# Moving squares instead of results in a masked depthwise convolution with GDN: denominators in 96x32 column groups

## The reference, cut to what matters

```python
pooled = x.mean(axis=(2, 3))
t = relu(batchnorm(pooled @ w1.T))
wt = (t @ w2.T + b2).reshape(b * 96, 1, 3, 3) * MASK      # rows above, and the pixel to the left
out = depthwise_conv(x, wt, padding=1) + bias             # one 3x3 filter per batch and channel
x2 = out * out
denom_sq = einsum('nchw,ic->nihw', x2, gamma_eff) + beta_eff
result = out * rsqrt(denom_sq)
```

## Time and profile before

| | us |
|---|---|
| median of 3 runs | 260.54 (258.8 to 266.99) |
| the profiled execution's own time | 260.12 |
| its span | 258.2 |
| busy: PE, DVE, ACT, POOL | 199.3, 204.8, 186.3, 169.7 |
| granted TensorE clock, mean | 0.945 |

### The profile page before, as it was taken

One profiled execution on the slowest core, in us unless ns is written; L12 is line 12 of the kernel. 1 busy time (PEld: TensorE's weight loads), 2 busy tenths in 40 slices (PEclk: granted clock), 3 DMA queues, 4 the chain that ended last, 5 costly groups with the idle time before them and its releaser, 6 DMA issues.

```text
span 258.2 us, 2123 instructions
## 1 busy us (share of the span) xinstructions
PE 199.3 (77%) x480; PEld 79.2 (31%) x480; DVE 204.8 (79%) x237; ACT 186.3 (72%) x203; POOL 169.7 (66%) x90
## 2 busy tenths in 40 slices
PE   0024221976999689999969899999698999999973
PEld 0021220322333333434324433333234333433220
DVE  6373239894599985999996699999959999999934
ACT  2220447693799568999974999999689866778472
POOL 2000000039597769899949699999499999999910
PEclk9999999995899959999995999999999999999967
DMA  7999999993429997987999989969835555566584
GB/s 204 243 245 240 243 241 240 244 243 121 143 82 223 309 284 258 300 242 227 262 323 285 274 280 290 271 213 255 307 109 164 176 164 162 150 187 187 148 254 131
DMA packets 13584, 57.63 MB, mean 223 GB/s; under 512 B 2595, under 2 KB 2598, under 8 KB 10886
## 3 DMA queue, kind: packets, MB, share of 16 engines
q1 hardware_dynamic: 13424, 57.22, 78.5%
q10 hardware_dynamic: 150, 0.29, 0.4%
HBM read 26.05 MB, written 25.17 MB: 198 GB/s over the span
## 4 chain that ended last, share of the span: by engine, by line
issue 38%; POOL 32%; DVE 13%; PE 8%; DMA 4%; ACT 2%; POOLq 0%; SPq 0%; ACTq 0%
POOL norm L585 26%; DVE acc L557 8%; POOL sq L574 6%; PE den L519 5%; DVE y L565 4%; DMA out_y<-norm 4%; ACT norm L427 1%; PE den L527 1%; PE acc L500 1%; ACT sq L405 1%; DVE y L567 0%; ACT norm L420 0%; DVE norm L733 0%; PE acc L501 0%; SPq L302 0%
## 5 line engine op out<-in xcount | busy, mean ns | idle before, releaser
L557 DVE SCALAR_TENSOR_TENSOR acc<-ximg,taps,acc 128x1016 f32<-128x1016 f32 x96 | 122.6, 1277 | 26.6 <-ACT acc L398 14.3
L585 POOL TENSOR_TENSOR norm<-y,norm 96x1024 f32<-96x1024 f32 x45 | 105.7, 2361 | 54.3 <-ACT norm L427 54.0
L519 PE MATMUL den<-sq,gam_e 96*96 96x512 f32 x252 | 124.7, 640 | 17.5 <-ACT norm L427 6.7
L427 ACT ACTIVATE norm<-den,beta_e 96x1024 f32<-96x1024 f32 x63 | 69.2, 1102 | 18.4 <-PE den L519 16.6
L519 PEld LDWEIGHTS den<-sq,gam_e 96*96 96x96 f32 x252 | 41.6, 174 | 91.1 <-issue 73.5
L500 PE MATMUL acc<-ximg,diag 128*128 128x512 f32 x108 | 58.3, 622 | 9.6 <-DVE y L567 9.6
L565 DVE SCALAR_TENSOR_TENSOR y<-ximg,taps,acc 128x1016 f32<-128x1016 f32 x48 | 61.1, 1273 | 1.7
L405 ACT ACTIVATE sq<-y 96x1024 f32<-96x1024 f32 x48 | 49.7, 1049 | 10.8 <-DVE y L567 10.7
L585 POOL TENSOR_TENSOR norm<-yd,norm 96x1024 f32<-96x1024 f32 x15 | 35.4, 2359 | 15.7 <-ACT norm L427 15.7
L368 ACT ACTIVATE pool_out<-ximg 128x1920 bf16 (+3 forms) x18 | 34.2, 1902 | 4.0 <-DMA ximg<-in_x 4.0
L574 POOL TENSOR_TENSOR sq<-yd 96x1024 f32<-96x1024 f32 x15 | 28.4, 1892 | 5.8 <-DMA yd<-y 5.8
(11 more groups left out here) (53 smaller groups left out, 46.5 us busy)
## 6 DMA issues: line engine op xcount, KB each, us to landing
out_y<-norm SPq DMA_DIRECT2D x63, 384.0 KB, 3.5
ximg<-in_x SPq DMA_DIRECT2D x12, 816.0 KB, 11.8
ximg<-in_x SPq DMA_DIRECT2D x8, 768.0 KB, 9.7
yd<-y SPq DMA_DIRECT2D x48, 128.0 KB, 3.7
ximg<-in_x SPq DMA_DIRECT2D x12, 272.0 KB, 12.6
ximg<-in_x SPq DMA_DIRECT2D x12, 256.0 KB, 9.7
ximg<-in_x SPq DMA_DIRECT2D x4, 720.0 KB, 6.9
out_y<-norm SPq DMA_DIRECT2D x2, 192.0 KB, 2.4
```

The lines of the kernel that those rows point to most:

```text
L427: nc.scalar.activation(norm[:, g], den[0:C, g % 2], ACT.Abs_reciprocal_sqrt, bias=beta_e[:, 0:1]).then_inc(normed, 1)
L519: ins = nc.tensor.matmul(den[0:C, g % 2, j:j + BANK], gam_e[:, :], sq[:, g, j:j + BANK], start=True, stop=True)
L557: nc.vector.scalar_tensor_tensor(out=tap_to(sums(u, s), tap), in0=tap_in(b, u, s, tap), scalar=tap_w(b, s, tap), in1=tap_to(sums(u, s), ta ...
L585: nc.gpsimd.tensor_tensor(norm[:, g], quarter(u, g), norm[:, g], ALU.mult).then_inc(scaled, 1)
```

## The change: what it does

- ACT squares each result as it stands in its block, on all 128 partitions, into `sq` (now six buffers). `move_d` then moves partitions 96 to 127 of the squares, not of the results, into `sqd`. The results stay where they are.
- The denominators of a block are formed in the block's own layout. For each half of 512 columns there are four matmuls with 32 output channels each: three from `sq` into partitions 0 to 31, 32 to 63 and 64 to 95 of `den`, and one from `sqd` with the 32 channels of this slot into partitions 96 to 127. Each has a weight of 96x32 and reads 512 columns.
- ACT's root (`beta_e` now one column per slot) and POOL's product then work on 128 x 1024 for 48 blocks, instead of 96 x 1024 for 64 quarters. POOL squares nothing. The store of a block is two DMAs, of 384 and of 128 KB.
- The written tables go. Each engine works through the blocks with fixed lags: in step n SP moves block n-1 and stores n-7, ACT squares n-1 and takes the root of n-5, PE forms the denominators of n-4. `norm` has six buffers. The last three products are on DVE. The start, the taps on DVE and the bases are the same work as before.

```diff
+SQUARE_LAG, MOVE_LAG, SUM_LAG, NORM_LAG, STORE_LAG = 1, 1, 4, 5, 7
+POOL_AT = {1: 0, 2: 1, 4: 2, 5: 3, 7: 4, 8: 5}
...
-        yd = sb("yd", [C, 2, N])
-        sq = sb("sq", [C, QUARTERS, N])
-        norm = sb("norm", [C, QUARTERS, N])
-        pool_out = sb("pool_out", [P, 2, (QR - CUT + 1) * W], BF16)
+        sq = sb("sq", [P, 2 * SLOTS, N])
+        sqd = sb("sqd", [C, 2, N])
...
-        beta_e = sb("beta_e", [C, 1])
+        beta_e = sb("beta_e", [P, SLOTS])
...
-        def move_d(sp, b, u, s):
-            sp.wait_ge(convolved, 2 * conv_no(b, u, s) + 2)
-            sp.dma_start(yd[s * CD:(s + 1) * CD, u % 2], y[C:P, u % 2, s]).then_inc(d_moved[u % 2], 16)
-        def store(sp, b, u, g):
-            sp.wait_ge(scaled, norm_no(b, u, g) + 1)
-            sp.dma_start(out_rows(b, u, g), norm[:, g]).then_inc(stored[g], 16)
...
+        def move_d(sp, n):
+            t, s = divmod(n, SLOTS)
+            sp.wait_ge(squared, n + 1)
+            if t >= 2:
+                sp.wait_ge(summed, (t - 2) * SLOTS + SLOTS)
+            sp.dma_start(sqd[s * CD:(s + 1) * CD, t % 2], sq[C:P, pair(n) * SLOTS + s]).then_inc(d_moved[t % 2], 16)
...
+        def store(sp, n):
+            b, u, s = place(n)
+            if n < ON_DVE:
+                sp.wait_ge(scaled, n + 1)
+            else:
+                sp.wait_ge(scaled_dve, n - ON_DVE + 1)
+            k = n % NORMS
+            r = s * QR + u * UR
+            sp.dma_start(out[b, :, r:r + UR, :].rearrange("c r w -> c (r w)"), norm[0:C, k]).then_inc(stored[k], 16)
+            r = SLOTS * QR + u * UR
+            sp.dma_start(out[b, s * CD:(s + 1) * CD, r:r + UR, :].rearrange("c r w -> c (r w)"),
+                         norm[C:P, k]).then_inc(stored[k], 16)
...
-        def square(act, b, u, g):
-            if above_zero(unit_no(b, u)):
-                act.wait_ge(summed, norm_no(b, u, g) - QUARTERS + 1)
-            act.wait_ge(convolved, 2 * conv_no(b, u, g) + 2)
-            nc.scalar.activation(sq[:, g], quarter(u, g), ACT.Square).then_inc(squared, 1)
...
-        def rsqrt(act, b, u, g):
-            act.wait_ge(summed, norm_no(b, u, g) + 1)
-            if above_zero(unit_no(b, u)):
-                act.wait_ge(stored[g], unit_no(b, u) * 16)
-            nc.scalar.activation(norm[:, g], den[0:C, g % 2], ACT.Abs_reciprocal_sqrt,
-                                 bias=beta_e[:, 0:1]).then_inc(normed, 1)
...
+        def square(act, n):
+            act.wait_ge(convolved, 2 * n + 2)
+            if n >= 2 * SLOTS:
+                act.wait_ge(summed, n - 2 * SLOTS + 1)
+            nc.scalar.activation(sq[:, pair(n) * SLOTS + n % SLOTS], result(n), ACT.Square).then_inc(squared, 1)
+        def rsqrt(act, n):
+            act.wait_ge(summed, n + 1)
+            if n >= NORMS:
+                act.wait_ge(stored[n % NORMS], 32 * (n // NORMS))
+            s = n % SLOTS
+            nc.scalar.activation(norm[:, n % NORMS], den[:, n % 2], ACT.Abs_reciprocal_sqrt,
+                                 bias=beta_e[:, s:s + 1]).then_inc(normed, 1)
...
-        def denominators(pe, b, u, g, last):
-            n = norm_no(b, u, g)
-            if g < SLOTS:
-                pe.wait_ge(squared, unit_no(b, u) * SLOTS + g + 1)
-            else:
-                pe.wait_ge(squared_d, unit_no(b, u) + 1)
-            if above_zero(n - 1):
+        def denominators(pe, n):
+            t, s = divmod(n, SLOTS)
+            pe.wait_ge(squared, n + 1)
+            pe.wait_ge(d_moved[t % 2], d_count(t))
+            if n >= 2:
                 pe.wait_ge(normed, n - 1)
-            if not last and (u, g) == (TAPS_UNIT, SLOTS):
-                pe.wait_ge(taps_ready, b + 2)
             if n == 1:
                 pe.wait_ge(taps_ready, 1)
+            k = pair(n) * SLOTS + s
             for j in range(0, N, BANK):
-                ins = nc.tensor.matmul(den[0:C, g % 2, j:j + BANK], gam_e[:, :], sq[:, g, j:j + BANK], start=True, stop=True)
+                for g in range(SLOTS):
+                    own = slice(g * CD, (g + 1) * CD)
+                    nc.tensor.matmul(den[own, n % 2, j:j + BANK], gam_e[:, own], sq[0:C, k, j:j + BANK], start=True, stop=True)
+                ins = nc.tensor.matmul(den[C:P, n % 2, j:j + BANK], gam_e[:, s * CD:(s + 1) * CD],
+                                       sqd[:, t % 2, j:j + BANK], start=True, stop=True)
             ins.then_inc(summed, 1)
...
-            if unit_no(b, u) >= 2:
-                dve.wait_ge(scaled, n_scaled(b, u, s))
-                dve.wait_ge(d_moved[u % 2], d_count(b, u) - 16 * SLOTS)
-            dst = y[:, u % 2, s]
-            nc.vector.scalar_tensor_tensor(out=tap_to(dst, LEFT), in0=tap_in(b, u, s, LEFT), scalar=tap_w(b, s, LEFT),
...
+            if n >= 2 * SLOTS:
+                dve.wait_ge(scaled, n - 2 * SLOTS + 1)
...
-        def square_d(pool, b, u):
-            pool.wait_ge(d_moved[u % 2], d_count(b, u))
-            nc.gpsimd.tensor_tensor(sq[:, SLOTS], quarter(u, SLOTS), quarter(u, SLOTS), ALU.mult).then_inc(squared_d, 1)
...
+            for n in range(BLOCKS + STORE_LAG):
+                if 0 <= n - MOVE_LAG < BLOCKS:
+                    move_d(sp, n - MOVE_LAG)
+                if 0 <= n - STORE_LAG < BLOCKS:
+                    store(sp, n - STORE_LAG)
...
+            for n in range(1, BLOCKS + NORM_LAG):
+                b, u, s = place(n)
+                k = n % PER_BATCH
+                if n + 1 < BLOCKS and on_act(n + 1):
+                    base_on_act(act, n + 1)
+                if k == HIDDEN_AT and b < B - 1:
+                    hidden(act, b + 1, n - SUM_LAG)
+                if n - SQUARE_LAG < BLOCKS:
+                    square(act, n - SQUARE_LAG)
+                if k == HIDDEN_AT and b < B - 1:
+                    read_taps(act, b + 1, n - SUM_LAG)
+                    diagonals(act, b + 1)
+                if 0 <= n - NORM_LAG:
+                    rsqrt(act, n - NORM_LAG)
+                if k in POOL_AT and b < B - 1:
+                    pool_on_act(act, b + 1, POOL_AT[k], "all", pools_before(b + 1, POOL_AT[k]))
...
+            for n in range(BLOCKS + SUM_LAG):
+                b, u, s = place(n)
+                chain = n % PER_BATCH == HIDDEN_AT and b < B - 1
+                if chain:
+                    hidden_sums(pe, b + 1, n - SUM_LAG)
+                if n + 1 < BLOCKS and not on_act(n + 1):
+                    base_on_pe(pe, n + 1)
+                if chain:
+                    tap_sums(pe, b + 1, n - SUM_LAG)
+                    pe.wait_ge(taps_ready, b + 2)
+                if n >= SUM_LAG:
+                    denominators(pe, n - SUM_LAG)
...
-                for u in range(UNITS):
-                    pool_unit(pool, b, u, False)
-            for u in range(UNITS - 1):
-                pool_unit(pool, B - 1, u, True)
+            for n in range(ON_DVE):
+                if n % PER_BATCH == HIDDEN_AT - NORM_LAG - 1 and place(n)[0] < B - 1:
+                    add_halves(pool, place(n)[0] + 1)
+                pool.wait_ge(normed, n + 1)
+                k = n % NORMS
+                nc.gpsimd.tensor_tensor(norm[:, k], result(n), norm[:, k], ALU.mult).then_inc(scaled, 1)
```

More of the change, by code:

```diff
@@ L116, in conv_gdn @@
     WAKING = 6
[L117 removed]
+    PE_SLOTS = (0, 2)
+    ON_DVE = BLOCKS - SLOTS
     flat = x.rearrange("b c h w -> b c (h w)")
[L119 removed]
+    assert P == 128 and N % BANK == 0
     ctx = ExitStack()
@@ L430, in act_unit @@
-        def act_unit(act, b, u, last, pools):
-            nb, nu = (b, u + 1) if u < UNITS - 1 else (b + 1, 0)
-            for what, g in ACT_STEPS[u]:
-                if what == "ahead":
-                    square(act, nb, nu, g)
-                elif what == "square":
-                    square(act, b, u, g)
-                elif what == "rsqrt":
-                    rsqrt(act, b, u, g)
-                elif what == "base":
-                    base(act, nb, nu, g)
-                elif what == "first" and not last:
-                    base(act, b + 1, 0, 0)
-                elif what == "pool" and pools:
-                    pool_on_act(act, b + 2 if u == UNITS - 1 else b + 1, g, g)
-                elif last:
-                    continue
-                elif what == "hidden":
-                    hidden(act, b + 1)
-                elif what == "taps":
-                    read_taps(act, b + 1)
-                    for s in PE_SLOTS:
-                        diagonal(act, b + 1, s)
@@ L455, in hidden_sum, with diagonals @@
-        def hidden_sum(s, sums, first, last):
-            return nc.tensor.matmul(hid_ps, w1r[:, s].rearrange("p t g -> p (t g)"), sums,
-                                    start=first, stop=last)
+            half = SLOTS * TAPS
+            nc.scalar.copy(taps[:, (b % 2) * half:(b % 2 + 1) * half], taps_in(n)).then_inc(taps_ready, 1)
+            act.wait_ge(taps_ready, b + 1)
+        def diagonals(act, b):
+            for s in PE_SLOTS:
```

(36 more changed lines are left out.)

324 lines of the change are left out of this document (92 added, 232 removed), and 8 rows, old and new, of tables (ACT_STEPS, SP_STEPS).

## The result

| us | before | changed |
|---|---|---|
| median | 260.01 (258.8 to 266.99, 4 runs) | 275.62 (271.13 to 278.25, 4 runs) |
| ratio to before | | 1.049 [1.035, 1.064] |
| profiled execution, its span | 260.1, 258.2 | 273.7, 271.9 |
| first and last result on DVE | 40.3, 244.6 | 40.2, 254.2 |
| lost between results | 21.5 | 31.2 |

The forecast was 251 us, faster. The time lies in the range (241 to 303), on the other side of no change. Some executions of a kernel had a lower granted clock over the whole run and took at least 1.5% longer than its fastest; ratios leave these out, and where most of a kernel's executions were such, only times are given.

What follows compares the result with a forecast made beforehand. DVE was taken to bound the kernel at 3.89 us a block: 40.3 start + 182.8 DVE + 7 stalls + 19 tail = 249.1, and 1.9 more, 251 us; range 241 to 303.

Steps and rivals of the forecast that it cites:

- the low end: PE: all four column groups stream at once, so a group of denominators costs 4 x 0.43 = 1.72 us.
- Both rivals on PE: Column groups overlap in pairs only, 3.44 us a group, 298 us, chance 0.28; or not at all, 6.88, 464 us, 0.18.
- The 2.1 that I took for issue: PE: a group's 16 records at 0.13 us each, the low end as issue allows it.
- the start: Before the first result on DVE: 40.3 us.
- DVE's 3.89: Steady part: DVE gives a result every 3.89 us where nothing is late, 47 intervals, 182.8 us.
- POOL and ACT: POOL: products of 2.36 us, 1.5 us free per block; ACT: 44.7 us a batch against 46.7 on DVE.
- the first unit: First unit: moved quarter there at 58.6, base of block 6 late, 3 us lost, within the 7 us of stalls.
- the tail: After the last result: move, three groups, root, product and store take 16.0 to 21.3 us, taken as 19, against 13.6.
- In the steady part this fits.: Transfers: a unit's last move, issued 1.1 us after its result, has 6.7 us to land; the median move took 3.7.
- The bytes are the same: Transfers: the change moves as many bytes as before; the new wait is for the moves of a whole unit.
- the moves hold PE in the loaded stretches: Rival: moves there take 12 us, three or four late units put back 16 to 21 us; 262 us, no change, chance 0.12.
- the 0.16 estimated: PE: a drain at each change of tiling mode, some 0.16 us, 9 us in all, lying in PE's slack.

Runs made afterwards that it cites:

- The fillers: The changed kernel with 12 useless bf16 matmuls on PE ahead of the wait for the moves of each unit but the first: 280.43 us (275.24 to 284.86).

## Why the prediction was wrong

The sum was 40.3 + 182.8 + 7 + 19 + 1.9 = 251. Measured: 40.2 + 182.8 + 31.2 + 17.7 + 1.8 = 273.7. One term is off, by 24.2 us; the others together by 1.5.

- **Right: PE.** Four column groups stream at once. The first records of the four start within 0.02 us of each other, the next four 0.43 later, four times: a group is 1.72 us, the low end.

```profile
149.98 0.63 PE L354 MATMUL den<-sq,gam_e 96*32 96x512 f32 x3
150.00 0.62 PE L355 MATMUL den<-sqd,gam_e 96*32 96x512 f32 x1
150.43 0.60 PE L354 MATMUL den<-sq,gam_e 96*32 96x512 f32 x3
150.45 0.59 PE L355 MATMUL den<-sqd,gam_e 96*32 96x512 f32 x1
```

  Both rivals on PE, 0.46 of the chance, were false: the second record of column group 0 stands in the queue ahead of the first record of group 1 and doesn't hold it. The 2.1 that I took for issue was too careful. The trace disagrees with the strict order that the Trainium skill gives in "TensorE: Matmul & The Clock Gate", "Part 3: Packing small matmuls", if that is taken across column groups, and 6.88/1.72 = 4.0 times is more than the 3.07 of its four row groups.
- **Right: the start, DVE's 3.89, POOL and ACT.** A product on 128 partitions took 2.37 us (2.36 forecast). Between results ACT's waits are for DVE and PE, and no base on ACT is late after the first.

```profile
L539 POOL TENSOR_TENSOR norm<-y,norm 128x1024 f32<-128x1024 f32 x45 | 106.4, 2367 | 135.1 <-ACT norm L296 135.1
L289 ACT ACTIVATE sq<-y 128x1024 f32<-128x1024 f32 x48 | 50.4, 1049 | 21.6 <-DVE y L380 21.4
```

- **Nearly right: the first unit and the tail, 3.7 us for 3 and 17.7 for 19.** Both are partly luck. In the first unit the moved squares were there at 59.2, near the 58.6 forecast, but the group and base behind them took 5.9 us, with the clock at half for a part of it, and DVE came 1.7 us later than forecast. In the tail the move landed in 2.3 us instead of 3.7, and the three groups took 7.0.
- **Wrong: "In the steady part this fits."** That step set 6.7 us of slack against the median landing of all moves, 3.7 us. Three things in it failed. *Issue:* the last move goes out 2.2 to 2.3 us after its result (3.3 where ACT has a sum in the way as well), not 1.1, since ACT's queue has a base ahead of the square. By itself this cost nothing that shows: with small loads it did no harm, and with the square first the moves landed no earlier. *Landing:* the moves that gated the three stalls took 7.3, 8.9 and 8.3 us, though the median of all fell to 2.4; most moves go in quiet stretches, where they took 2.2 to 2.4. I had read "The bytes are the same" and not that the change puts three pieces in a row, 455 GB/s by the sizes on the page. *What a late move costs:* I priced it at its lateness. But PE worked at half its clock behind the idle time, and group and base took 7.3 us for 4.2, so a group late by 2.2 us cost 5.4.
- **The rival "the moves hold PE in the loaded stretches"** was the right mechanism: it named the stretches, the queue and PE's wait. It had 0.12, and 12 - 6.7 = 5.3 us for each of three or four units, 262 us. Three stalls of 5.4, 7.2 and 5.6 us were there, 18.2 in all, against the 18 of its sum. That these sizes agree is luck: it took a landing of 12 us and no cost of the clock, and the runs show 7.3 to 8.9 us and nearly half of the 18.2 from the clock. Its total was off because the sum holds nothing else. The first unit (3.7), one more stall of 2.1 near 88 us at the first filter change, the 4.8 for POOL at the filter changes and small ones (2.4) make the other 13.
- **What stays open.** What the clock alone is worth, by an experiment: the split by rows gives it 8.7 of the 18.2 us and 1.7 of the first unit's 3.7. The fillers bought the clock at a price of their own, and in the run without the wait it fell as well, at the filter change. And why the runs of one kernel differ by 3% with the clock granted.

## What to carry to other kernels

When a wait is added for a transfer, compare its slack with the landing in the fullest stretch, which the bytes issued per unit against the GB/s carried at full share hint at; the median over the kernel says nothing on it. Price the lateness with the work behind it at the clock that PE has after an idle time. Count the slack from where the transfer is issued in fact, behind all that stands ahead of its producer. More lag alone gave nothing that shows (273.6 us) while more was issued than carried, and spreading the bytes alone did half (265.7); together they made the change pay (254.8, against 260.4 before).

## What was not expected of the hardware

- Each 32-column group of TensorE works through its own records: four start within 0.08 us whichever of two orders they are queued in, also for f32 with its two records.
- A change of tile width costs 0.09 to 0.17 us between f32 records (0.95 to 1.03 us for 0.86), which agrees with the drain that the Trainium skill names in "TensorEngine Tiling (Array Packing)", "Key Properties", near the 0.16 estimated. (The prediction's "0.43 is hidden" is a slip: records of 0.59 us start 0.43 apart, so 0.16 is what overlaps.) Widths 96 and 32 didn't run side by side in that kernel, though their outputs are apart.
- Moves on a queue of their own beside a full one landed in 3.5 us at the median and 9.3 at most. Those that gate a unit were 1 to 3 us quicker than in the same queue (4.9 to 7.6 us), and still far from the 2.2 of a quiet stretch.
- The granted clock was 0.50 in a stretch where PE was 96% busy (126 to 132 us of the kernel without the wait), behind 12 records of small matmuls with 0.8 and 0.3 us of idle time around them, so an idle time of 3 us, as in the changed kernel, isn't needed for a fall. In the changed kernel it had also fallen before one of the three waits: it was 0.50 already from 161.5 to 164.7.
